# Attention pairs on one core: where the two maximum tiles and the transposition of the maxima stand

## The reference, cut to what matters

```python
q1 = heads(x @ Q1_w.T); k1 = heads(x @ K1_w.T + K1_b)      # 8 heads of 32
q2 = heads(x @ Q2_w.T); k2 = heads(x @ K2_w.T + K2_b)
v  = heads(x @ V_w.T)
a1 = softmax(q1 @ k1.T / scale);  a2 = softmax(q2 @ k2.T / scale)
attn = a1 - lam * a2
o = attn @ v                                               # then group norm, out_w
```

## Time and profile before

| what | value |
|---|---|
| median of 3 runs | 6543.28 us (6539.59 to 6547.5) |
| profiled execution, its own time | 6535.96 us |
| its span, first to last instruction | 6533.1 us |
| granted TensorE clock, mean | 0.970 |
| busy: PE, PEld, DVE, ACT, POOL | 93%, 60%, 72%, 47%, 47% |

### The profile page before, as it was taken

How to read it: one execution, slowest core, us unless ns; L and a number is a source line. 1 busy time by engine, 2 the same in 40 slices (tenths; PEclk the granted TensorE clock), 3 DMA queues, 4 the chain that set the end, 5 groups by cost and what they waited for, 6 DMA issues and landing times.

```text
span 6533.1 us, 125913 instructions
## 1 busy us (share of the span) xinstructions
PE 6063.3 (93%) x41498; PEld 3899.9 (60%) x41498; DVE 4700.7 (72%) x6535; ACT 3089.8 (47%) x5470; POOL 3092.9 (47%) x1382
## 2 busy tenths in 40 slices
PE   6999999899999999999999999999999999999998
PEld 4565565655656566565665656556565565655656
DVE  5767777676776767767677676776767767677676
ACT  4535445354453544535445354453544535355353
POOL 3706437074470734707347073471725617256271
PEclk9999999999999999999999999999999999999999
DMA  2202122121221212212022120221202212021120
GB/s 77 49 27 52 32 47 45 31 51 28 48 45 30 53 29 45 45 29 58 25 48 48 28 54 24 50 47 28 59 19 51 47 32 55 18 55 43 37 54 17
DMA packets 111217, 271.38 MB, mean 42 GB/s; under 512 B 34000, under 2 KB 56656, under 8 KB 102096
## 3 DMA queue, kind: packets, MB, share of 16 engines
q1 hardware_dynamic: 110544, 262.73, 17.4%
HBM read 23.38 MB, written 16.78 MB: 6 GB/s over the span
## 4 chain that ended last, share of the span: by engine, by line
PE 82%; DVE 10%; ACT 3%; issue 3%; DMA 1%; SPq 0%; DVEq 0%; ACTq 0%
PE psum L1033 19%; PE psum L853 17%; PE psum L985 15%; PE psum L964 14%; PE psum L1087 5%; PE psum L992 5%; DVE minus_max L614 2%; PE psum L1057 2%; PE psum L1012 1%; DVE small L550 1%; ACT probs L411 1%; PE psum L1117 1%; DVE max_rows L623 1%; DVE max_rows L624 1%; DMA stack<-stage 1%
## 5 line engine op out<-in xcount | busy, mean ns | idle before, releaser
L329 POOL TENSOR_TENSOR prob_sums<-probs 128x1024 f32<-128x1024 f32 x752 | 1795.2, 2387 | 3207.9 <-ACT probs L411 2923.4
L411 ACT ACTIVATE probs<-psum 128x512 f32<-128x512 f32 x4096 | 2222.9, 595 | 1419.9 <-PE psum L1033 1408.0
L614 DVE TENSOR_REDUCE minus_max<-psum 128x1 f32<-128x1024 f32 x2048 | 2422.4, 1209 | 398.6 <-PE psum L964 391.7
L1033 PE MATMUL psum<-stack 98*128 98x512 f32 x4096 | 1479.5, 438 | 43.9 <-ACT probs L411 41.7
L964 PE MATMUL psum<-stack 96*128 96x512 f32 x4096 | 1241.3, 412 | 106.0 <-DVE max_rows L624 64.9
L329 POOL TENSOR_TENSOR prob_sums<-prob_sums,probs 128x1024 f32<-128x1024 f32 x512 | 1220.2, 2383 | 101.5 <-ACT probs L411 62.6
L1033 PEld LDWEIGHTS psum<-stack 98*128 98x128 f32 x4096 | 704.9, 190 | 737.3 <-ACT probs L411 480.2
L985 PE MATMUL psum<-probs,v_tokens 128*32 128x256 f32 x16384 | 1112.2, 388 | 0.0
L964 PEld LDWEIGHTS psum<-stack 96*128 96x128 f32 x4096 | 721.5, 191 | 409.2 <-DVE max_rows L624 171.2
L853 PE MATMUL psum<-act_hi,w_hi 128*128 128x512 f32 x1728 | 713.7, 413 | 62.0 <-DVE minus_max L614 48.3
L985 PEld LDWEIGHTS psum<-probs,v_tokens 128*32 128x32 f32 x16384 | 429.4, 109 | 465.8 <-issue 288.9
(11 more groups left out here) (141 smaller groups left out, 4744.7 us busy)
## 6 DMA issues: line engine op xcount, KB each, us to landing
stack<-stage SPq DMA_DIRECT2D x1024, 128.0 KB, 3.0
stack<-stage SPq DMA_DIRECT2D x256, 256.0 KB, 3.1
x_tile<-x_dram SPq DMA_DIRECT2D x17, 1024.0 KB, 4.8
x_tile<-o_head SPq DMA_DIRECT2D x512, 32.0 KB, 1.8
stack<-max_rows SPq DMA_DIRECT2D x512, 4.0 KB
y_dram<-residual SPq DMA_DIRECT2D x16, 512.0 KB, 2.8
y_dram<-stage SPq DMA_DIRECT2D x16, 512.0 KB, 3.7
stage<-w_split_dram SPq DMA_DIRECT2D x1, 3848.0 KB, 12.5
```

Of the source, the lines that this page charges most:

```text
L329: nc.gpsimd.tensor_tensor(total, first, probs[:, k % NP, :], ALU.add).then_inc(sum_pool, 1)
L411: nc.scalar.activation(probs[:, k % NP, half * HALF:(half + 1) * HALF], ps[:, 4 + half, :], ACT.Exp).then_inc(p_ready, 1)
L614: v.tensor_reduce(nm[:, u % 2, q:q + 1], flat_in, AX.X, ALU.max, negate=True).then_inc(ring_free, 1)
L1033: mm(ps[:, 4 + half, :], stack[0:KS, s, 1, kt * P:(kt + 1) * P], stack[0:KS, s, 0, half * HALF:(half + 1) * HALF], start=True, stop=True). ...
```

## The change

In the lists, the turn moves from the front to between the two maximum tiles. On TensorE one maximum tile stands between the exponent tiles of a pair; the turn stands behind the second exponent tile, then the weighted values and the sum with ones; the other maximum tile and then the projection come last. VectorE takes the first maximum tile and the turn, then its first share of other work, then the second maximum tile and the projection. ScalarE reads a projection behind the first tile's exponentials of the next pair, no longer of the same pair. SyncE gets one more wait, before the key rows of unit 8. The counts of all computing instructions stay.

```diff
@@ -94,13 +94,11 @@
     beside = {}
     for u in range(UNITS):
         for pair in range(PAIRS):
-            beside[u, pair] = [("turn", u + 1)] if 2 * pair == 2 * NT - AHEAD and u + 1 < UNITS else []
-            for kt in (2 * pair, 2 * pair + 1):
-                n = u * NT + kt + AHEAD
-                if n < UNITS * NT:
-                    beside[u, pair].append(("score", *divmod(n, NT)))
-            if (u, pair) in PROJ_BESIDE:
-                beside[u, pair].append(("proj", 4 + PROJ_BESIDE.index((u, pair))))
+            scores = [("score", *divmod(n, NT)) for n in range(u * NT + 2 * pair + AHEAD, u * NT + 2 * pair + AHEAD + 2)
+                      if n < UNITS * NT]
+            turn = [("turn", u + 1)] if 2 * pair == 2 * NT - AHEAD and u + 1 < UNITS else []
+            proj = [("proj", 4 + PROJ_BESIDE.index((u, pair)))] if (u, pair) in PROJ_BESIDE else []
+            beside[u, pair] = scores[:1] + turn + scores[1:] + proj
     return before, beside
 
 
@@ -249,6 +247,9 @@
                         if u < 2:
 
                             sp.wait_ge(ring_free, b * len(RING) + RING_AT["proj", t] + 1)
+                        elif u == NT and t == 1:
+
+                            sp.wait_ge(ring_free, b * len(RING) + RING_AT["proj", 5] + 1)
                         elif u >= NST and t == 2 * m:
 
                             sp.wait_ge(st_full, b * 2 * UNITS * NT + (u - NST + 1) * 2 * NT)
@@ -410,14 +411,14 @@
                             act.wait_ge(st_full, b * 2 * UNITS * NT + 2 * k + half + 1)
                             nc.scalar.activation(probs[:, k % NP, half * HALF:(half + 1) * HALF],
                                                  ps[:, 4 + half, :], ACT.Exp).then_inc(p_ready, 1)
-                        for item in BESIDE[u, kt // 2] if kt % 2 == 0 else []:
-                            if item[0] == "proj":
-                                if item[1] == 4:
-
-                                    for s in range(NST):
-                                        done = len(range(s, 8, NST))
-                                        act.wait_ge(stack_in[s], (b * SLOT_USES[s] + done) * STACK_DMAS * 16)
-                                project(item[1])
+                        pair_before = divmod(u * PAIRS + kt // 2 - 1, PAIRS)
+                        if kt % 2 == 0 and pair_before in PROJ_BESIDE:
+                            if pair_before == PROJ_BESIDE[0]:
+
+                                for s in range(NST):
+                                    done = len(range(s, 8, NST))
+                                    act.wait_ge(stack_in[s], (b * SLOT_USES[s] + done) * STACK_DMAS * 16)
+                            project(4 + PROJ_BESIDE.index(pair_before))
                 def norm_coefficients(t):
 
                     act.wait_ge(g_var, b * CT + t + 1)
@@ -711,14 +712,13 @@
                     ring_step(item)
                 for u in range(UNITS):
                     for pair in range(PAIRS):
-                        kt = 2 * pair
-                        for item in BESIDE.get((u, pair), []):
+                        items = BESIDE[u, pair]
+                        for item in [it for it in items if it[0] == "turn" or it == items[0]]:
                             ring_step(item)
-                            if item[0] == "score":
-                                beside_score(u, kt)
-                                kt += 1
-                        for at in range(kt, 2 * pair + 2):
-                            beside_score(u, at)
+                        beside_score(u, 2 * pair)
+                        for item in [it for it in items[1:] if it[0] != "turn"]:
+                            ring_step(item)
+                        beside_score(u, 2 * pair + 1)
                         if (u, pair) == NORM_AT:
                             norm_sums(0)
                 norm_variance(0)
@@ -1033,9 +1033,12 @@
                                 mm(ps[:, 4 + half, :], stack[0:KS, s, 1, kt * P:(kt + 1) * P],
                                    stack[0:KS, s, 0, half * HALF:(half + 1) * HALF], start=True,
                                    stop=True).then_inc(st_full, 1)
-                            if kt % 2 == 0:
-                                for item in BESIDE[u, pair]:
+                            for item in BESIDE[u, pair][:1] if kt % 2 == 0 else []:
+                                if item[0] == "score":
                                     ring_step(item)
+                        for item in BESIDE[u, pair]:
+                            if item[0] == "turn":
+                                ring_step(item)
                         if (u, pair) == (NORM_AT[0], NORM_AT[1] + 1):
                             norm_groups(0)
                         if k >= 2:
@@ -1043,6 +1046,9 @@
                         weighted(*divmod(k - 1, NT))
                         for late in ones_after(u, pair):
                             add_up(*late)
+                        for item in BESIDE[u, pair][1:]:
+                            if item[0] != "turn":
+                                ring_step(item)
                 weighted(UNITS - 1, NT - 1)
                 add_up(UNITS - 1, 1)
```

## The result

The changed kernel takes 6859.38 us (median of 4 runs, 6852.43 to 6865.68) against 6542.74 before: a ratio of 1.0483, 95% interval 1.0468 to 1.0498. Slower, as forecast, by 317 us where 347 were forecast. Its span is 6857.7 us, 324.6 more than before.

A forecast was written before the change was run, and what follows sets the result against it. ScalarE was taken to set the stretch between exponent tiles, TensorE the rest; 18.4 + 0.65 + 0.13 + 2.7 = 21.9 us an image, times 16 = 350 on 6536, gave 6886, 6890 with the median's 7 us; range 6760 to 6970.

The forecast's parts named there:

- What bounds a pair: Between a pair's two exponent tiles: ScalarE sets the length, so maximum tiles there cost nothing; room for two, hardly more.
- Second maximum tile: Moved behind the weighted values, where TensorE had no wait: 0.46 us in each of 40 pairs, 18.4 us an image.
- Turn pair: Pair with the turn moved behind the second exponent tile: 4.12 us, 0.05 more than now; 13 pairs give 0.65.
- The 0.13 for the turn of unit 14: That turn lies in a covered stretch now; moved out of it, it was to cost 0.13 us an image.
- Projections: Five pairs at the projections: ring waits raise them from 35.1 to 37.8 us, 2.7 more; bounds 33.5 and 41.
- Sum: All terms of an image together: 21.9 us more, times 16 images 350 us on the profiled execution's 6536.
- The clock: Rival: idle TensorE time in each pair drops a quarter of 58 pairs to the lower clock, 7120 us; chance 0.06.
- Half hidden: Rival: earlier first half and idle time before weight loads absorb half the moved tile, 6680 us; chance 0.08.
- The gain alone: Rival: moved tile finds room behind the weighted values, turn pairs fall by 0.41 us, 6465 us; chance 0.05.
- VectorE's pace: Condition of the rival "The gain alone": VectorE, not TensorE, paces a pair, if its work there exceeds 3.1 us.

The follow-up runs named there:

- e3: Changed kernel with the first maximum tile of every pair, between the exponent tiles, issuing its two matmuls twice: 6867.07 us.
- e9: Changed kernel with ScalarE computing exponentials for only half of the columns of each exponent tile, from an image's fifth tile on: 6458.09 us.
- e10: Kernel before the change with ScalarE computing exponentials for only half of the columns of each exponent tile, from an image's fifth tile on: 6449.5 us.
- e1: Changed kernel with the second maximum tile of every pair issuing only one of its two matmuls: 6676.2 us.

## Why the prediction was right, step by step

- *What bounds a pair.* Right. That the unit without maximum tiles was as fast as one with two told that the stretch was ScalarE's. e3, e9 and e10 show it.
- *Second maximum tile, 0.46 us in 40 pairs, 18.4 us.* The size was nearly exact: 4.00 less 3.53, 3.57 less 3.10, so 0.47. But two of the 40 are the image's first pairs, which took 4.14 and 4.45 us before and take 4.02 and 4.13 now, 0.44 less together. So the plain pairs give 17.3 instead of 18.4. These two means mix two levels of the clock. The first row is the kernel before at the start of the second image, the second row the changed kernel:

```profile
499.60:509.80 10.20, 10.01 (x40) 5.08 (x39) 5.40 (x5) 3.85 (x9) 4.71 (x2) 0.50 0.01 2
523.90:530.60 6.70, 6.70 (x28) 3.60 (x30) 4.21 (x4) 3.69 (x8) 3.82 (x2) 0.50 0.01 2
```

The granted clock is 0.50 in both. Such a start is found in nine of the 16 images before, 10.2 us long, and in eight now, 6.8 us long in seven of them. In images that start at the full clock the two pairs take 3.39 and 3.26 us before, 3.13 and 3.57 now: there too the moved tile costs next to nothing, 0.05 us in the two together. Why that is so at the start of an image stays open.
- *Turn pair, 0.05 more.* It takes 4.12 us to the hundredth, but the single pair that I read in the earlier trace rows, 4.07, was that of one of the shorter units: before, the turn pair of units 2, 8 and 11 takes 4.09, of the others 4.20, of the first 4.37, and the 13 have a mean of 4.19. The term is about 0.9 us an image below zero where I had 0.65 above. This was a term mis-sized by reading one pair for all. The 0.13 for the turn of unit 14 is not there either: its pair takes 3.53 before and 3.54 after.
- *Projections, 2.7 us more.* Measured 4.0, from both ends: before they took 34.0 as a mean, not 35.1, because the low clock falls in five of the 16 images only, and after 38.05, where 37.8 was worked out. The ring's waits are in the chain as followed:

```profile
1033.27 2.77 PE psum L853 x12
...
1037.29 1.04 ACT stage L386
...
1038.35 1.23 DVE stage L610
...
1039.63 0.37 PE psum L970
...
1051.86 4.61 PE psum L853 x12
```

ScalarE's read and VectorE's behind two exponentials, then the turn, which waited for them; and a run of 12 matmuls at the lower clock. The sum for the undisturbed case was too high (36.8 in the seven images without a dip), and the clock made it up: that the mean came out near 37.8 is luck. What was mis-sized is the start, 35.1 for 34.0, read from one image with a dip.
- *Sum.* 17.3 less 0.9, plus 4.0, is the measured 20.4 us an image, where 21.9 were forecast; 16 x 1.5 = 24 of the 31 us by which the forecast was high. The rest is that I put the median 7 us above the profiled execution, as before, and now it is 1 us below it. The sum is nearer than its terms: three were too high by 1.1, 1.5 and 0.1 us, and one too low by 1.3.
- *The clock.* Behind the first pairs of an image it holds in the plain and turn pairs and sags at the projections alone:

```profile
1040.00:1050.00 10.00, 9.17 (x62) 5.11 (x61) 4.68 (x7) 3.06 (x5) 2.67 (x2) 0.87 0.13 32
1050.00:1060.00 10.00, 8.60 (x44) 5.32 (x44) 4.49 (x6) 2.98 (x5) 2.10 (x2) 0.83 0.30 63
...
1150.00:1160.00 10.00, 10.00 (x82) 5.26 (x70) 8.18 (x11) 4.94 (x10) 7.50 (x4) 1.00 0.42 93
```

The last row is a stretch of plain and turn pairs, in each of which the second exponent tile takes some 0.5 us longer than its matmuls (0.97 instead of 0.47) because its weights wait. The section "A second HAM failure mode" of the Trainium skill (TensorE: Matmul & The Clock Gate) warns of idle moments between groups; here they did no harm in the pairs. At the projections TensorE sat idle for longer before the clock fell, 1.68 us ahead of the turn and 1.21 ahead of the projection at the low clock:

```profile
1039.63 0.37 PE L970 MATMUL psum<-w_full,minus_max 128*8 128x128 f32 x1 [1.68 <-DVE stage L610]
...
1051.86 0.50 PE L853 MATMUL psum<-act_hi,w_hi 128*128 128x512 f32 x1 [1.21 <-DVE minus_max L615]
```

The same idle times stand in all 16 images, and in seven of them no fall follows, so these waits alone do not decide it and what does stays open.

- *The rivals.* Half hidden fell with e1. The gain alone fell with the result and with e1, where VectorE's work stayed and the time fell by 183 us; its saving in the turn pairs is real, though: they fell from 4.19 to 4.12 us although the moved tile adds its 0.47 to them. VectorE's pace would decide it only if its work passed the pair's length, and its idle time doubled instead.

## What to carry to other kernels

Before moving work on the engine that seems full, find out what ends the stretch it leaves and what ends the stretch it goes to: work that hides behind another engine's time is free there, and behind a stage in which its engine has no wait it costs its full length, 0.47 us of 0.47 here. A stage of the same loop that lacks this work, such as the last unit of a pipeline that has run dry, is an experiment that the trace has already made. And read the mean over a loop, not one instance: first iterations, clock dips and units that differ made up most of what the forecast missed.

## What the runs showed beyond that

- A busy share of matmuls can rise in a slower kernel: 93% to 94%, while weight loads fell from 60% to 57%.
- The name of who was waited for can mislead. In the timeline of the changed kernel the exponentials of the turn's pair are put down to GpSimd:

```profile
1095.83 2.37 POOL L330 TENSOR_TENSOR prob_sums<-probs 128x1024 f32<-128x1024 f32 x1 [1.94 <-PE psum L992]
...
1098.28 2.37 POOL L330 TENSOR_TENSOR prob_sums<-prob_sums,probs 128x1024 f32<-128x1024 f32 x1
...
1100.22 0.63 PE L1033 MATMUL psum<-stack 98*128 98x512 f32 x2
...
1100.65 0.60 ACT L412 ACTIVATE probs<-psum 128x512 f32<-128x512 f32 x1 [1.73 <-POOL prob_sums L330]
```

The first exponential of that pair needs the sum of the unit's tiles 0 and 1, which GpSimd ended at 1098.20, 2.4 us earlier; the addition that ended at 1100.65 is one that it does not need. It starts 0.43 us behind its exponent matmul, as the one of the pair before does (0.44), so by these times the matmul released it and GpSimd's end fell on the same moment.
- Two exponentials out of PSUM, one behind the other, take 0.66 us at 128x256 and 1.08 at 128x512. A single one takes 0.38 and 0.60, so the second starts some 0.28 and 0.48 us behind the first.
